# Whole-array edge rows of 896, one-block setup and softmax, and gathers written out one by one, in a four-layer GNN on one core

## The reference, cut to what matters

```python
# block 0: mean of the neighbours, then a linear layer
h = segment_sum(x[src], dst) / deg;  x = norm(x + h @ W.T + b)
# block 1: two SAGE layers, then graph attention, then relations of four kinds
e = leaky_relu(al_src[src] + al_dst[dst], 0.2)          # two heads, loops added
m = segment_max(e, dst);  ex = exp(e - m[dst])
alpha = ex / segment_sum(ex, dst)[dst]
out = segment_sum(alpha[:, :, None] * h[src], dst)
agg = segment_mean(xt[etype, src], dst * 4 + etype)     # a mean for each relation
# block 2: an edge MLP with batch norm over all edges, summed by source node
# block 3: sum over edges of edge_weight * x @ W[etype], eight relations
```

## Time and profile before

| what | value |
|---|---|
| median of 3 runs | 9854.47 us (9854.09 to 9855.87) |
| the profiled execution | 9853.46 us |
| its span, first to last instruction | 9851.7 us |
| POOL busy | 7073.0 us (72%) |
| PE busy | 6580.5 us (67%) |
| DVE busy | 5043.2 us (51%) |
| mean granted TensorE clock | 0.663 of full speed |

### The profile page before, as it was taken

The page is one execution under the profiler, slowest core; times in us unless marked ns, Lnnn a source line. Parts: engine busy times, 40 slices in busy tenths (PEclk is TensorE's granted clock), DMA queues, the critical chain, the costliest instruction groups (busy, mean ns, idle before and its releaser), DMA issues. The chain is left out here.

```text
span 9851.7 us, 143700 instructions
## 1 busy us (share of the span) xinstructions
PE 6580.5 (67%) x30272; PEld 5016.5 (51%) x30272; DVE 5043.2 (51%) x16370; ACT 1313.1 (13%) x3288; POOL 7073.0 (72%) x8234
## 2 busy tenths in 40 slices
PE   2777755666688888841888856666566667876665
PEld 1656643333566664521777734444455556743333
DVE  7676654443455542665777734444422225744445
ACT  0000000000000002730000010000222225720000
POOL 1777777777777777776777777777377776737775
PEclk9666555555655668555999975555677778975555
DMA  1211112222333332001777742332366665532222
GB/s 52 52 46 49 48 29 58 52 52 52 92 104 104 104 99 87 5 11 29 220 220 219 219 107 56 60 60 55 93 185 185 185 185 140 151 119 52 52 52 53
DMA packets 663097, 934.86 MB, mean 95 GB/s; under 512 B 278665, under 2 KB 441076, under 8 KB 662636
## 3 DMA queue, kind: packets, MB, share of 16 engines
q0 software_dynamic: 273312, 613.35, 23.6%
q1 hardware_dynamic: 389708, 320.66, 11.2%
HBM read 790.44 MB, written 143.03 MB: 95 GB/s over the span
## 5 line engine op out<-in xcount | busy, mean ns | idle before, releaser
L784 PE MATMUL sage_window<-sage_hot,sage_message 128*128 128x128 f32 x4992 | 1479.4, 437 | 664.7 <-DMA sage_message<-t_x,sage_index_stage 321.0
L784 PE MATMUL block_window<-block_hot,block_message 128*128 128x128 f32 x3328 | 1196.1, 460 | 721.2 <-DMA block_message<-t_rel,block_index_stage 335.0
L784 PEld LDWEIGHTS sage_window<-sage_hot,sage_message 128*128 128x128 f32 x4992 | 1100.3, 299 | 1043.8 <-issue 728.8
L784 PEld LDWEIGHTS block_window<-block_hot,block_message 128*128 128x128 f32 x3328 | 796.5, 297 | 1093.2 <-issue 618.0
L699 DVE TENSOR_TENSOR first_acc<-first_acc,sage_window 128x128 f32 (+1 forms) x1664 | 591.6, 356 | 982.3 <-PE sage_window L784 979.0
L596 POOL DMA_INDIRECT block_message<-in_x,block_index_stage x832 | 853.8, 1026 | 237.5 <-issue 222.0
L1965 POOL DMA_INDIRECT eh_message<-t_q,eh_stage x880 | 832.1, 946 | 251.9 <-issue 232.5
L784 PE MATMUL gat_window<-gat_hot,gat_message 128*128 128x128 f32 x6656 | 849.7, 281 | 183.7 <-DVE gat_hot L604 93.2
L596 POOL DMA_INDIRECT gat_message<-t_h,gat_index_stage x832 | 793.3, 953 | 237.5 <-issue 222.0
L596 POOL DMA_INDIRECT sage_message<-t_s,sage_index_stage x832 | 789.0, 948 | 237.5 <-issue 222.1
L596 POOL DMA_INDIRECT rgcn_message<-t_rel,rgcn_index_stage x832 | 788.7, 948 | 237.5 <-issue 222.1
(11 more groups left out here) (485 smaller groups left out, 10839.6 us busy)
## 6 DMA issues: line engine op xcount, KB each, us to landing
eh_window<-t_p SPq DMA_DIRECT2D x880, 64.0 KB
t_hidden<-eh_hidden SPq DMA_DIRECT2D x110, 512.0 KB, 3.0
sc_rows<-t_hidden SPq DMA_DIRECT2D x110, 512.0 KB, 3.6
eh_low_rows<-t_low SPq DMA_DIRECT2D x110, 256.0 KB, 3.5
t_rel<-n_h SPq DMA_DIRECT2D x49, 512.0 KB, 2.6
eh_message<-t_q,eh_stage POOLq DMA_INDIRECT x880
block_message<-in_x,block_index_stage POOLq DMA_INDIRECT x832, 2.5
sage_message<-t_x,sage_index_stage POOLq DMA_INDIRECT x832, 2.5
```

The lines of the kernel that those rows point to most:

```text
L784: last = nc.tensor.matmul(ps[k][:, b, :], message[u][:, f:f + P], hot[:, u, j * P:(j + 1) * P], start=(j == 0), stop=(j == heads - 1))
```

## The change

It has four parts.

1. The edge arrays are loaded with 896 consecutive edges in a partition row (`EW`), so 119 of the 128 rows hold edges and a tile is one of seven pieces of a row. `by_block` puts the pieces back in tile order when they are turned; tile numbers stay as they were.
2. `constants`, `segment_masks` and the seven blocks of `edge_setup` become one block. The counts of the relations leave it. POOL pads three buffers, ACT loads the edge weights and attributes and takes 14 of the 20 PSUM copies. The load of `x` moves into block 0's pass.
3. The whole softmax becomes one block with classes `RunTotals` and `Runs`. A total is made by a forward scan, then a backward scan (maximum) over its result, and the correction across rows works on 128 ends in place of 896. The counts of the four relations and their reciprocal are made here. `attention_terms` loads `dst` and the kinds again ahead of its own work.
4. The gathers of the six passes and of `edge_hidden` are written out, 832 and 880 instructions, and take their index column from the full array. ACT's copies, the staging buffers, the carriers and POOL's loops are gone.

```diff
+EW = EB * P
-PLACES = [("degrees", 28), ("block0", 80), ("sage1", 42), ("sage2", 165), ("attention", 275), ("softmax_masks", 18), ("softmax_dst", 42),
-          ("softmax_top", 24), ("softmax_sum", 24), ("softmax_self", 12)]
+PLACES = [("degrees", 28), ("block0", 80), ("sage1", 42), ("sage2", 165), ("attention", 275), ("softmax", 85)]
...
-        @block.scalar
-        def _(act):
-            with act.Fori(0, ITERS, 1) as it:
-                for h in range(2):
-
-                    act.wait_ge(e.half_used[h], half0 + it)
-                    nc.scalar.copy(stage[h][:], index[:, bass.ds(it * U + h * HU, HU)]).then_inc(e.staged, 1)
-
         @block.gpsimd
         def _(pool):
-            with pool.Fori(0, ITERS, 1) as it:
+            for it in range(ITERS):
                 for u in range(U):
                     h, k = divmod(u, HU)
-                    if k == 0:
-
-
-                        pool.wait_ge(e.carried, staged0 + it * 2 + h)
-                        pool.wait_ge(e.staged, staged0 + it * 2 + h + 1)
-                        nc.gpsimd.tensor_tensor(m.carrier[:], m.ones_i[:], m.ones_i[:], ALU.add).then_inc(e.carried, 1)
+                    if k == 0 and half0 + it > 0:
+                        pool.wait_ge(e.half_used[h], half0 + it)
                     pool.indirect_dma_start(message[u][:], None, table,
-                                            bass.IndirectOffsetOnAxis(ap=stage[h][:, k:k + 1], axis=0)).then_inc(e.gathered[u], 16)
+                                            bass.IndirectOffsetOnAxis(ap=index[:, it * U + u:it * U + u + 1], axis=0)).then_inc(e.gathered[u], 16)
...
+        @block.gpsimd
+        def _(pool):
...
+            nc.gpsimd.memset(raw[:, 1:4], 0).then_inc(padded, 1)
+            nc.gpsimd.memset(weight[:], 0.0).then_inc(padded, 1)
+            nc.gpsimd.memset(ea[:], 0.0).then_inc(padded, 1)
...
+            act.wait_ge(padded, 3)
+            load_edges(act, ea, a["edge_attr_2"].rearrange("e k -> (e k)"), 2, ea_in)
+            load_edges(act, weight, a["edge_weight"], 1, weight_in)
...
+            sp.wait_ge(ints_padded, 2)
+            for k, name in enumerate(("dst", "edge_type_4")):
+                load_edges(sp, m.edge_ints[:, k], a[name], 1, ints_in)
+            sp.wait_ge(ints_in, 96)
             with sp.Fori(0, T // (AQ * QU), 1) as it:
...
+        @block.gpsimd
+        def _(pool):
+            place_records(nc, m, pool, later_records(m, "softmax"), *PLACED["softmax"], placed)
+            pool.wait_ge(self_kept, 16)
+            for j in range(NT):
+                pool.indirect_dma_start(rows_got[:, j, :], None, m.t_self,
+                                        bass.IndirectOffsetOnAxis(ap=m.last_edge[:, j:j + 1], axis=0)).then_inc(got, 16)
...
+            for r in range(R4):
+                steps(ts(kind, kind_of[:], float(r), None, ALU.is_equal))
+                steps.settle()
+                steps(counts.forward(ahead, prev, kind))
+                steps.settle()
+                steps(counts.back(work[:, r], next_, ahead))
+                steps.settle()
...
+            for r in range(R4):
+                steps(ts(kind, kind_of[:], float(r), None, ALU.is_equal))
+                steps.settle()
+                steps(nc.vector.copy_predicated(w[:], kind.bitcast(I32), work[:, r]))
+                steps.settle()
+            nc.vector.reciprocal(w[:], w[:]).then_inc(w_ready, 1)
...
+            nc.vector.reciprocal(top, total)
...
+            stt(self_weight.rearrange("p e k -> p k e"), own[:], 0.5, top, ALU.mult, ALU.mult).then_inc(self_ready, 1)
+            stt(e[:], e[:], 0.5, top, ALU.mult, ALU.mult).then_inc(alpha_ready, 1)
+            dve.wait_ge(got, 16 * NT)
...
-            with pool.Fori(0, ITERS2, 1) as it:
+            for it in range(ITERS2):
                 for u in range(U):
-                    h, k = divmod(u, HU)
-                    if k == 0:
...
+                    if u % QU == 0 and it >= 1:
+                        pool.wait_ge(made[u // QU], it)
```

More of the change, by code:

```diff
@@ L132, in constants @@
[L132 to L167, removed]
@@ new lines, in _ @@
+        @block.tensor
+        def _(pe):
+            pe.wait_ge(ident_ready, 1)
+            pe.wait_ge(dst_ready, 1)
+            for b in range(EB):
+                nc.tensor.transpose(row[:, b * P:(b + 1) * P], dst[:, b * P:b * P + 1], m.ident[:]).then_inc(base_turned, 1)
+            for i, (n, b0, b1) in enumerate(work):
+                source, ready, _ = turns[n]
+                pe.wait_ge(*ready)
+                if i >= 4:
+                    pe.wait_ge(*taken(i - 4))
+                for b in range(b0, b1):
+                    last = nc.tensor.transpose(ps[i % 4][:, b - b0, :], source[:, b, :], m.ident[:])
+                last.then_inc(turned, 1)
@@ L1540, in attention_softmax @@
[L1540 to L1561 removed]
+        sb, pb, sem = place(nc, ctx, "softmax")
@@ new lines, in attention_softmax @@
+        own, dst, self_weight = m.e, at_dst[:, 0], spread[:].rearrange("p e k -> p (e k)")[:, 0:2 * EW].rearrange("p (e k) -> p e k", k=2)
+        top, total = at_dst[:, 0:2], at_dst[:, 2:4]
+        ps = [pb(f"turn{k}", [P, 4, P]) for k in range(2)]
+        rows, cols = [pb(f"run_rows{k}", [4, 2, 2, P]) for k in range(3)], [pb(f"run_cols{k}", [P, 2, 2, 4]) for k in range(3)]
+        runs = Runs(nc, sb, sem, 4, rows[0][:, 0])
+        counts = RunTotals(nc, sb, sem, "counts", R4, rows[1][:, 0], cols[0][:, 0])
@@ new lines, in _, with turn @@
+        @block.tensor
+        def _(pe):
+            def turn(first, last):
+                for i in range(first, last):
+                    n, b0, b1 = turn_work[i]
+                    source, ready, _ = turns[n]
+                    if ready:
+                        pe.wait_ge(*ready)
+                    if i >= 2:
+                        pe.wait_ge(kept, i - 1)
+                    for b in range(b0, b1):
+                        last_one = nc.tensor.transpose(ps[i % 2][:, b - b0, :], source[:, b, :], m.ident[:])
+                    last_one.then_inc(turned, 1)
+            turn(0, 4)
+            runs.turn(pe, m.ident[:])
+            counts.turn(pe, m.ident[:])
+            spreads.turn(pe, m.ident[:])
+            counts.turn_back(pe, m.ident)
+            spreads.turn_back(pe, m.ident)
+            turn(4, 6)
+            tops.turn(pe, m.ident[:])
+            tops.turn_back(pe, m.ident)
+            sums.turn(pe, m.ident[:])
+            sums.turn_back(pe, m.ident)
+            turn(6, 10)
@@ new lines, in _, with keep @@
+        @block.scalar
+        def _(act):
+            def keep(first, last):
+                for i in range(first, last):
+                    n, b0, b1 = turn_work[i]
+                    act.wait_ge(turned, i + 1)
+                    nc.scalar.copy(turns[n][2][:, b0:b1, :], ps[i % 2][:, 0:b1 - b0, :]).then_inc(kept, 1)
+            keep(0, 4)
+            keep(4, 6)
+            for n, t in enumerate((e, own)):
+                act.wait_ge(shifted, n + 1)
+                nc.scalar.activation(t[:], t[:], ACT.Exp).then_inc(raised, 1)
+            keep(6, 10)
```

671 lines of the change are left out of this document (295 added, 376 removed).

## The result

The changed kernel takes 9593.94 us (median of 4 runs, 9591.39 to 9597.13) beside 9855.17 us for the kernel before in the same runs (4 runs, 9854.09 to 9856.15). The profiled execution took 9594.82 us, with a span of 9592.9.

A forecast was written before the change was run, and what follows sets the result against it. Gather passes were taken as POOL-paced, setup and softmax as DVE chains with barriers, the stage behind gat as POOL's alone. -153 - 110 + 45 + 33 - 4 = -189 from 9853.5 gave 9664.5, stated as 9666, range 9630 to 9710.

The forecast's parts named there:

- Setup, -153: Start to first gather: shorter chain brings the first gather from 186.22 to 33 us, 153 less, bounds 138 and 156.
- the lower of the two bounds: POOL's padding of 5376 columns in setup: 4.8 us at DVE's memset price, against 24.8 at POOL's tensor_scalar price.
- Softmax, -110: Softmax start to gat's first gather: 324.0 to 214 us, POOL's scatters setting the node gathers' start; bounds 100 and 120.
- Behind gat, +45: Stage behind gat, set by POOL alone: 35 more scatters at 1.27 us, 44.6 us with no cover.
- Logits' stage, 0: Logits' stage: look-ups start about 8.7 us later behind a new load, but POOL's last scatter covers the delay.
- the cover of 8.7 us: Logits' stage: time from the look-ups' end to POOL's last scatter, said to hide the delay with 1 to 2 us spare.
- Starts, -4: Five later starts without ACT's copy in front, 0.7 us less each, 4 us in all.
- Written-out gathers, +33: Six passes and edge_hidden: fetch gaps add 90 us, removed loop costs save 56.5, net 33 slower.
- The first half of this term, -56.5: Six passes and edge_hidden: carriers, their waits and loop branches go, 8.0 us a pass and 8.5 in edge_hidden.
- the second half, +90: Passes and edge_hidden: a code fetch every 113 instructions, 1.56 us each, 2.76 in gat, adding 90 us.
- fetches are hidden: Rival for the written-out gathers: code fetches cost nothing, so they give -56.5 and the time is 9576; 13%.

The follow-up runs named there:

- e6: Kernel before with only its gathers written out, usual chip: 9794.20 us beside 9846.94, ratio 0.9947.
- e7: Changed kernel with its gathers back in loops, usual chip: 9644.89 us, ratio 0.9792 to the kernel before.
- e9: Changed kernel, semaphore batches altered in three scatter stages, 12 memsets ahead of DVE's scatter-by-source loop, slow chip; no total given, scatter by source 349.3 us.
- e11: Changed kernel with only 12 one-element memsets added ahead of DVE's loop in the scatter by source: 9588.45 us, ratio 0.9733 to the kernel before.
- e1: Kernel before with only its gathers written out, slow chip: 12057.83 us beside 12320.82, ratio 0.9780.
- e4: Changed kernel with 35 scatters moved back from gat's stage to the softmax, slow chip: 11852.82 us, ratio 0.9618 to the kernel before.
- e5: Changed kernel run again unaltered, usual chip: 9588.62 us, ratio 0.9738 to the kernel before.

## Why the prediction was wrong, and where it was right

**Setup, -153: right to 0.2 us.** POOL's memsets took 2.3, 0.8 and 1.6 us and were done at 5.7; the padding was near the lower of the two bounds, as chosen. That the sum is right to 0.2 is luck: DVE's copies end at 30.7 and the record store, issued at 25.5, lands at 31.2, where 30 was put, and from there to the first gather it takes 1.8 us and not 3.0.

**Softmax, -110: measured -104.8, inside the bounds.** The mechanism held: POOL's 85 scatters, not DVE, set the node gathers' start. The rows, in time:

```profile
4147.24 0.36 SPq L1392 DMA_DIRECT2D softmax_spread<-t_last  x1
...
4173.40 8.74 POOL L605 DMA_INDIRECT t_rec<-attention_records,all_position  x1 [0.30 <-issue]
4173.60 7.75 DVE L1271 TENSOR_TENSOR_SCAN softmax_at_dst<-softmax_same,softmax_spread 128x896 f32<-128x896 f32 x4
...
4275.23 0.35 SPq L1394 DMA_DIRECT2D t_self<-softmax_spread  x1
...
4296.11 0.97 POOL L605 DMA_INDIRECT t_rec<-attention_records,all_position  x1 [0.31 <-issue]
4298.97 0.99 POOL L1387 DMA_INDIRECT softmax_rows<-t_self,all_last_edge  x1 [1.89 <-issue]
...
4366.40 0.94 POOL L382 DMA_INDIRECT gat_message<-t_h,all_src  x1 [6.49 <-ACTq L321]
```

DVE issued the self weights at 128 us, 6 sooner than its sum said; POOL was ready at 151.7, 6 later than 145.5. The price of a scatter beside DVE's work was the term that was too low: by 4278.3 the first 70 had taken 130.4 us, 1.86 each, where 78 in 134, 1.72 each, were put. A good part of that is one scatter: it was busy for 8.74 us, until DVE's four scans without a gap between them (7.75 us) were over. Without it 69 took 121.4 us, 1.76 each, close to what was put. Beside the 1792-wide reciprocal of 11.35 us they took 1.27 each, and so did the other 15, as forecast.

**Behind gat, +45: right** (+46.9). The gap is in both kernels and no part of it. From first to last scatter it takes 44.4 us more, 1.27 for each of the 35; POOL's DRAIN, 3.73 us in place of 0.87, adds 2.9 that the forecast did not have.

**Logits' stage, 0: right.** The look-ups' last copy starts at 4140.13 and POOL's last scatter at 4140.46; the cover of 8.7 us was used up to the last 0.3.

**Starts, -4: they gave 0.9.** Behind gat, where the rows can be parted, POOL's way from the barrier to rgcn's first gather went from 1.06 to 0.79 us: the copy on ACT was worth 0.3 there, not 0.7.

**Written-out gathers, +33: wrong; -55.9.** The first half of this term, -56.5 for carriers, waits and branches, was right: -55.9 in the changed kernel's trace and -50.9 in e6's, and the totals of e6 and e7 moved by 52.7 and 56.3. The failed step is the second half, +90: "I read them as the fetch of further code". The written-out gathers have no such gap, so it is 0. Three gaps of the same size fitted, but the distance was misread: from the 114th to the 226th scatter it is 112 and not 113, seven batches of 16, so that a scatter with its batch's waits took 1.283 us (1.27 is the plain step). And the rows of before already spoke against it. In each stage the gap stands at the 114th scatter of that stage's own list, whether 49 other DMAs stand ahead of it (logits) or none (sage2, gat), while a period in the code would fall at another place in each. I took a distance for the law and did not ask from where it counts. The probes then showed that the gap goes with the batches of semaphores. The rival "fetches are hidden", 9576, was the right one, and had 13%. The Trainium skill (Runtime: NRT & Kernel Launch, Instruction fetch mechanics) had told this case: code in a straight line is fetched at a cost that is mostly hidden. This trace agrees, with no gap above 0.32 us inside the passes in 5872 gathers, but for one wait for PE at the second turn of block0's and of gat's pass.

**What no term held: +11.2 behind edge_hidden.** 5 of it are the end of edge_hidden: its gathers now end 11 us sooner, but the loads of windows and stores that SP issues do not, and after the last gather SP still issues for 30 us. That they come with the written-out gathers e6 and e7 show; that SP's queue is the cause is read from the trace and was not tried. 7 are the slower loop turn, and e9 and e11 show that it goes with what stands ahead of DVE's loop; whether by the place of the code or by the moment of the start is not shown. Without these 11 and with the softmax as forecast, the hidden case's 9576 would have been met within 2 us (9593.9 - 11.2 - 5.2 = 9577.5).

## What to carry to other kernels

When a gap in one stretch is to be carried over to other code, count from where it repeats in each stretch, and ask which of the things that differ (batches, semaphores, direction) the new code shares; here one look at "the 114th of each list" would have parted code from batch. Where one engine is last in each stage, work moved between stages gives nothing, as with POOL's 35 scatters. And an idle time that is removed in the middle of a stage is not yet a gain: follow it to the stage's end. The removed gaps, and part of the early node gathers, came back in POOL's DRAIN, which shows in no group of busy time and in no wait. Writing a loop out is worth its carriers, branches and waits, some 8 us per 832 gathers here, if the engine is the one that sets the pace.

## What the runs showed of the hardware that was not expected

- A loop's turn can cost 0.13 us more or less with what stands ahead of another engine's loop: 12 small memsets on DVE took the stage from 355.9 to 349.4 us and the next one from 171.9 to 176.1.
- One chip of those used was slower. The kernel before took 9847 us on some and 12207 to 12321 on that one, at the same granted clock (0.66 to 0.67) and with POOL's DMAs still 1.25 us apart where they do not wait. What differs is the time of DVE, PE and ACT between instructions, inside the passes and outside: of the 2267 us between the profiled spans of e1 and e6, the same kernel, 1507 lie in the passes and edge_hidden and 406 in the logits' stage, where DVE's longest wait for nothing that the profile shows is 35 us against 0.3. DVE's waits in 900 us of sage1 in e4 (slow chip), then in 830 us of it in e5:

```profile
DVE first_acc L485 <- issue: 263.1, 160, 3.9
DVE sage_hot L393 <- issue: 218.1, 163, 6.8
DVE first_acc L485 <- remote: 76.8, 51, 3.8
```

```profile
DVE first_acc L485 <- PE sage_window L570: 434.4, 622, 1.0
DVE sage_hot L393 <- issue: 63.6, 84, 0.9
```

  The columns are total us, times and the longest. On the slow chip DVE waits for nothing that the profile shows, for up to 6.8 us. Why is not known. The change is worth more there: ratio 0.962 in e4 against 0.974.
- A gap at the 114th indirect DMA of a list comes with semaphores that change every 8 or 16 and not with 24, 32 or 64. It is 1.66 to 1.70 us in most places, and 1.66 to 3.26 behind sage2. Removing it brought no time, since POOL's DRAIN at the end of the block grows by 0.0815 us for each DMA that is then not yet settled.
- A scatter that POOL issues beside scans on DVE can be held until the scans are over: one took 8.74 us beside four of them without a gap, where 0.97 is the rule, and none was held beside a reciprocal of 11.35 us.
